# Two graph layers on one core: each adjacency block in two transfers, and the kept sums back in seven

## What is computed

```
h  = relu(layernorm(x))
s  = (h @ W) @ a1 ;  t = (V @ W) @ a2
e  = leaky_relu(s[:, None] + t[None, :], 0.2), where adj > 0, else -9e15
x1 = x + elu(softmax(e, axis=1) @ V + h)
h2 = relu(layernorm(x1))
out = x1 + relu((adj^T @ h2) @ U.T / column_sums(adj)[:, None])
```

## Time and profile before

| | us |
|---|---|
| median of 3 runs (lowest, highest) | 379.76 (377.72, 380.29) |
| the profiled execution, its own time | 379.21 |
| its span, as the trace has it | 377.4 |
| mean granted TensorE clock | 0.959 of full |

### The profile page before, as it was taken

How to read it: one execution, slowest core, us unless ns; L and a number is a source line. 1 busy time by engine, 2 the same in 40 slices (tenths; PEclk the granted TensorE clock), 3 DMA queues, 4 the chain that set the end, 5 groups by cost and what they waited for, 6 DMA issues and landing times.

```text
span 377.4 us, 16296 instructions
## 1 busy us (share of the span) xinstructions
PE 304.1 (81%) x7582; PEld 280.0 (74%) x7582; DVE 302.5 (80%) x410; ACT 257.4 (68%) x323; POOL 117.6 (31%) x120
## 2 busy tenths in 40 slices
PE   1927766657778777777888999999979999999995
PEld 0812655556667766677788999888969999999995
DVE  7899999797999558888997879999969876402965
ACT  2222799779999789698999899997767787101000
POOL 8866387388140382030106103003101110401000
PEclk9977699889999899899999999999999999999999
DMA  9999999999999999997101002000321000510211
GB/s 164 137 111 106 110 107 111 137 107 109 109 110 139 104 109 105 103 102 82 58 3 34 24 24 80 24 24 25 129 59 30 5 3 3 112 31 2 55 33 30
DMA packets 27961, 27.88 MB, mean 74 GB/s; under 512 B 22169, under 2 KB 23129, under 8 KB 27766
## 3 DMA queue, kind: packets, MB, share of 16 engines
q0 software_dynamic: 4752, 16.90, 43.1%
q1 hardware_dynamic: 20982, 9.39, 10.0%
q10 hardware_dynamic: 2160, 0.56, 0.8%
HBM read 74.08 MB, written 3.43 MB: 205 GB/s over the span
## 4 chain that ended last, share of the span: by engine, by line
PE 38%; DVE 25%; ACT 22%; issue 9%; DMA 4%; POOL 1%; SPq 1%; DVEq 0%; POOLq 0%
DVE scratch L895 15%; PE w L1248 12%; ACT q L745 10%; PE q L1335 9%; ACT arena L727 9%; PE q L1221 8%; DVE arena L947 5%; PE w L1335 4%; DMA bi<-rows_sb 3%; ACT arena L731 3%; PE w L1120 1%; DMA buf_a<-in_L_gnn_a_dram 1%; PE w L1294 1%; POOL buf_a L517 1%; SPq L420 1%
## 5 line engine op out<-in xcount | busy, mean ns | idle before, releaser
L1248 PE MATMUL w<-v_sb,arena 128*61 128x65 f32 (+1 forms) x4224 | 158.7, 225 | 7.9 <-issue 6.5
L895 DVE CUSTOM_DVE_ANT_0 scratch<-adj_sb,t_row 125x2048 uint8<-125x2048 uint8 x66 | 152.9, 2317 | 1.5
L1248 PEld LDWEIGHTS w<-v_sb,arena 128*61 128x61 f32 (+1 forms) x4224 | 143.6, 140 | 9.7 <-issue 7.6
L1221 PE MATMUL q<-bi,adj_sb 128*64 128x125 bf16 x2112 | 95.8, 226 | 38.8 <-ACT q L745 27.2
L1221 PEld LDWEIGHTS q<-bi,adj_sb 128*64 128x64 fp8e4 x2112 | 71.4, 113 | 53.6 <-ACT q L745 36.3
L727 ACT ACTIVATE arena<-q,t_col 128x1000 f32<-128x1000 f32 (+2 forms) x102 | 88.4, 870 | 7.5 <-PE q L1221 7.4
L731 ACT ACTIVATE arena<-arena,t 128x1000 f32<-128x1000 f32 (+2 forms) x58 | 63.6, 1096 | 23.2 <-DVE arena L947 22.6
L947 DVE SCALAR_TENSOR_TENSOR arena<-arena,b_col,q 128x1000 f32<-128x1000 f32 (+1 forms) x43 | 52.3, 1224 | 19.4 <-PE q L1221 14.6
L745 ACT ACTIVATE q<-second_row,minus_b 128x750 f32<-128x750 f32 (+1 forms) x49 | 47.9, 977 | 1.1
L745 ACT ACTIVATE q<-arena,minus_b 128x375 f32<-128x375 f32 (+1 forms) x53 | 42.3, 800 | 1.3
L1335 PE MATMUL q<-g_all,adj_sb 124*128 124x129 f16 (+1 forms) x588 | 34.8, 220 | 0.0
(11 more groups left out here) (144 smaller groups left out, 229.6 us busy)
## 6 DMA issues: line engine op xcount, KB each, us to landing
adj_sb<-in_adj_dram POOLq DMA_DIRECT2D x33, 500.0 KB, 39.3
t_row<-saved_dram SPq DMA_DIRECT2D x1, 1290.0 KB, 7.2
saved_dram<-x_sb SPq DMA_DIRECT2D x6, 193.5 KB, 1.9
arena<-s_dram SPq DMA_DIRECT2D x2, 500.0 KB, 7.2
out_dram<-v_sb SPq DMA_DIRECT2D x10, 96.0 KB, 1.8
x_sb<-in_x_dram SPq DMA_DIRECT2D x1, 928.0 KB
v_sb<-x_dram SPq DMA_DIRECT2D x1, 768.0 KB, 5.7
v_sb<-n_L_gnn_entity_embs_dram ACTq DMA_DIRECT2D x2, 256.0 KB, 5.6
```

The source lines that it names most:

```text
L895: nc.vector.tensor_tensor_reduce(out=junk[0:R, :], in0=adj_bytes[0:R, b, half], in1=t_row[0:R, half], scale=1.0 / ONE, scalar=0.0, op0=ALU ...
L1221: last = nc.tensor.matmul(q[n % Q_SLOTS][e:e + width, bank, start:start + R], weights, bi[:, i % BI_SLOTS, k, :], start=not ON_ACT[n] and ...
L1248: last = nc.tensor.matmul(att(i)[e0:e1, bank, place_in, :], e[:, k * R + e0:k * R + e1], v_sb[:, c, :], start=(c == 0 and place_in == 0), ...
```

## The change

There are two parts. `load(b)` issues two transfers for a block, each of 125 rows by 2048 columns, one behind the other, both counting on `adj_in[b]`; the guard waits for 32 there. And the kept sums come back by seven transfers, one for each saved piece, each behind its own tile of the last group: SP waits until `weighed` shows 2, 6, 10, 14, 18, 22 and 26 tiles of group 4. DVE waits for all seven at the fifth output.

```diff
+    LOAD_TILES = (2, 6, 10, 14, 18, 22, 26)
...
             sp.wait_ge(r1_ready, NI)
-            sp.dma_start(saved, saved_dram).then_inc(part_loaded, 16)
+            for k, o in enumerate(AHEAD):
+                first, size = k * 3 * (2 * D + 1), (OUTS[o][1] - OUTS[o][0]) * (2 * D + 1)
+                sp.wait_ge(weighed, NC * (NI - 1) + LOAD_TILES[k])
+                sp.dma_start(saved[:, first:first + size], saved_dram[:, first:first + size]).then_inc(part_loaded, 16)
...
                 pool.wait_ge(ones_set, b + 1)
-                nc.gpsimd.dma_start(adj_sb[0:R, b, :], adj[first_row(b):first_row(b) + R, :]).then_inc(adj_in[b], 16)
+                for h in range(2):
+                    half = slice(h * HALF, (h + 1) * HALF)
+                    nc.gpsimd.dma_start(adj_sb[0:R, b, half], adj[first_row(b):first_row(b) + R, half]).then_inc(adj_in[b], 16)
...
                 if h == 0:
-                    dve.wait_ge(adj_in[b], 16)
+                    dve.wait_ge(adj_in[b], 32)
...
                     if o == AHEAD[0]:
-                        dve.wait_ge(part_loaded, 16)
+                        dve.wait_ge(part_loaded, 16 * len(AHEAD))
```

## The result

The changed kernel takes **380.67 us** (median of 20 runs, 379.62 to 382.07), the kernel before 378.79 (20 runs, 376.88 to 381.38): a ratio of 1.0052, 95% interval 1.0036 to 1.0068. It is half a per cent slower, about 1.9 us. The forecast was 376.6 us, a gain. The profiled execution took 381.01 us, its span is 379.2 against 377.4.

What follows compares the result with a forecast made beforehand. The prediction took the chain's small transfers and PE instruction fetches, delayed behind adjacency loads, as the cost, not the adjacency rate. Halves -1.0 and reloads -2.0 made -3.0 us: about 376.6 us as a median, 8-in-10 range 373.5 to 381.

Steps and rivals of the forecast that it cites:

- The price of an issue: On POOL, each block's one more adjacency issue was taken to cost 0.52 us, the median of 33 issues.
- The rival of cheaper issues: On POOL, a half's issue costs half, 0.26 us; gain near 5.8 us, time 374 us; chance 0.12.
- the two slower ones: POOL's dearer issues or full queue (issues from 0.9 us: 384 to 386, chance 0.08); a gap per transfer (to 386.5, chance 0.04).
- Blocks 7 to 12 ... Hidden: Six more issues, +3.1 us, ahead of POOL's 37.20 instruction: it comes at 38.8, lasts 0.6, before its DVE reader at 39.84.
- Blocks 21 to 28 ... 99.35: Eight more issues, 4.2 us, ahead of POOL's sum at 94.30: DVE's wait for it ends at 99.35 instead of 94.87.
- The step that issues bi is +2.5: After group 1's scores, the step issuing group 2's shifts transfer (bi) comes 2.5 us late, against 4.5 at the scores of 122.19.
- If waits go by packets, the 3.9 us becomes 1.95: Small shifts transfer (bi) under adjacency loads: half-size packets halve its extra wait, so it takes 3.7 us instead of 5.67.
- ... and a fetch comes some 1 to 2 us sooner. Of the five stalls, four hang on this edit: PE's stalls of 1.66, 1.06, 2.27 and 0.98 us under adjacency loads, read as late instruction fetches, were to go with halves.
- The new wait for group 2's product: DVE near 145: blocks 29 to 32 add four issues, 2.1 us, so POOL's product ends at 147.5 and DVE waits 2.3.
- Edit 2: Kept sums reloaded by seven transfers instead of one: PE's stall at 274.70 goes, -2.0 us, at no cost.
- edit 1: Adjacency blocks loaded as halves: shorter waits for shifts and fetches against POOL's extra issues, about -1.0 us at 175 us.
- The rival by bytes: Waits go by bytes, so halves don't shorten them; POOL's 2.5 us delay stays, edit 2 gives 2.0: 380.3 us; chance 0.22.

Runs made afterwards that it cites:

- The kernel with U's power early: Changed kernel with the power of U's columns put ahead of adjacency blocks 11 and 12, running sum left behind block 28: 379.46 us, ratio 1.0011 to the kernel before.
- 376.44: Changed kernel with POOL's running sum of group 0 put ahead of block 23, U's power left behind block 12: 376.44 us, ratio 0.9922 to the kernel before.
- The traffic kernels: Kernel before with twelve adjacency blocks loaded again during group 3, by whole rows, halves or quarters: 395.11, 391.43 and 390.30 us, one execution each.
- the two kernels at 375.00 and 377.82: 375.00: changed kernel, U's power ahead of block 11, group 0's sum ahead of block 23. 377.82: kernel before, whole blocks, seven reloads, sum ahead of block 23.

## Why the prediction was wrong

**The price of an issue** was right: 0.52 us for a half, 66 of them. The rival of cheaper issues fell, and so did the two slower ones: no issue was longer than 0.74, and DVE waited 0.7 us in all for a block.

**"Blocks 7 to 12 ... Hidden"** was the first step that failed. The power of U was to come at 38.8 and last 0.6; it came at 39.64 and lasted 2.30, so its reader on DVE is 2.1 us late. Begun at 37.2 or 38.0, ahead of the guard, it lasts 0.57 or 0.58. The difference is the guard of 39.22 to 41.49 beside it: POOL's operation ends 0.45 us after it, at 41.94. The Trainium skill ("SBUF — State Buffer", SBUF: two separate sides) says that VectorE, in an operation with two SBUF inputs, and GpSimd, in one that reads SBUF, share a pair of ports by an exclusive lock: who starts first has it to the end, the other waits in full. The trace agrees, 2.30 against 0.57 us. The same befell the first power (20.65, 1.24 us instead of 0.88, under the guard that began at 18.86), so that place gave +0.7 and not +0.3. I had taken both durations from rows where nothing lay beside them and moved them under a guard. The kernel with U's power early shows its price: 1.5 us at the shifts of group 2, 1.2 us in the medians (379.46 against 380.67, from different rounds).

**"Blocks 21 to 28 ... 99.35"**: the mechanism was right, eight issues in front of a sum that DVE waits for, and it is the main loss (5.3 us of lag at group 2's shifts when it stands alone, 4.2 us of time by the medians 380.67 and 376.44). The size was off by the step above: POOL's power at 72.27 waits for DVE, and inherits its 2.1 us. I had called the eight issues ahead of it hidden by 6.89 us of idle time, which they were; the lag of its releaser I had not carried. 94.87 + 2.1 + 4.1 = 101.1, as measured.

**"The step that issues bi is +2.5"**: measured +4.9. Of this 1.7 us is the lag just told; the scores of 130.68 did recover 2.0 us, as forecast, but the copy of the shifts on ACT behind them is 0.6 later than they are.

**"If waits go by packets, the 3.9 us becomes 1.95"** was the step on which the gain rested, and it was mis-sized: 3.9 became 3.2 (4.91 - 1.75). My own fit had a slope, 0.64 us a packet, and a constant, "some three of them once" (by that slope 3.9 - 4 x 0.64 = 1.3 us), and I halved both. The traffic kernels, one execution each, show that a part of about 2 us stays whatever the packets are. By the slope alone, 4 packets of 0.27 us, the gain would have been 1.1 us; it was 0.8.

**"... and a fetch comes some 1 to 2 us sooner. Of the five stalls, four hang on this edit"** failed outright, and this is where the forecast gain was lost. I had carried the rule for small transfers to PE's stalls without a row of one at another packet size. The reading as late fetches was right, and the page does show the blocks, of which I wrote that no row does (59 instruction packets of 16 KB). But a fetch comes no sooner: its packet begins 3.7 us after PE has entered the instruction block before it, with whole blocks and with halves, and PE takes 6.04 and 6.05 us for 256 instructions. So the stalls of group 2 stay at 1.46, 2.00 and 0.97 us. Nor could I count them off the chain one by one: where the supply of instructions sets the pace, a stall won comes back at a later one, and a lag stays (+4.3 us at instruction block 12, +4.2 at block 20). The new wait for group 2's product did come (148.68), with 1.1 us instead of 2.3, since DVE was itself late. Group 2's start was to be +0.9 and was +4.1; the end of group 2 was to be -1.0 and was +4.0.

**Edit 2** was right in size, -2.0 against -2.2 in the combined kernel and -2.3 alone, and its price nothing; the stores behind it on SP's queue cost nothing. Its reason was half right: the stall belonged to the load, but the waits for tiles did not count. The 2.0 us was one trace's figure; behind the one reload the other traces have stalls of 0.6 to 2.1 us, or none, by where the fetch falls.

**The sum.** Forecast: edit 1 -1.0, edit 2 -2.0. Measured: +4.0 and -2.2. (The median was also 0.2 us too low by its own sum: 379.76 - 3.0 is 376.8.) The rival by bytes came nearest in number, 380.3, but not by its ledger: it had the shifts +2.5 late with no gain in latency and nothing given back. That the halves save 2 us and more once POOL's order is mended, it denied; the two kernels at 375.00 and 377.82 show it.

## What to carry to other kernels

Splitting transfers costs an issue each on the engine that issues them: look for what that engine's later instructions release, and write it ahead of the loads in the same edit. Here that turned +0.5% into -1.1%. When a step is late, carry its lag through every engine that it releases before calling later work hidden; and when an operation slides to another time, look at what now runs beside it, for its duration is that of the old neighbourhood. A latency fitted as slope and constant scales only by its slope. And before a stall with no releaser is put into a sum, look in the trace for what ends it and how often that comes: here one instruction packet per 256 instructions of PE, every 6 us under the load.

## What the runs showed of the chip that I had not expected

- A 64 x 1 operation of POOL takes 0.57 us when it starts ahead of a guard of DVE, 2.30 when it starts 0.4 us behind one.
- Halving packets from 0.55 to 0.28 us takes the two small shift transfers from between 5.3 and 6.3 us down to between 4.8 and 5.1; of the wait of a 500 KB load about 2 us is left at any packet size tried.
- PE's stalls with no releaser are late instruction fetches: all 166 end 1.2 to 1.6 us after a packet of 16,384 bytes on the instruction queue, at the same place in a count of 256 instructions.
- While POOL's queue is full, PE gets 256 instructions in 6.0 to 6.1 us with packets of 0.55, 0.28 or 0.15 us; in group 3, with that queue empty, it takes 4.6 us for them and does not wait.
- One transfer of 1290 KB from a hardware queue (packets of 10,320 bytes) holds up a fetch that falls into its first 1.2 us: the instruction packet begins 2.9 to 4.5 us after PE enters the instruction block before it. With seven of the same bytes (packets of 1548 bytes), issued within 4.2 us, it begins after 1.6 to 1.8, and PE does not stall.
